# Low-rank attention with layer norm and experts on one core: the query and key weights loaded, turned and absorbed ahead of the first rows

## The reference, cut to what matters

```python
c_q  = h_t @ W_DQ + b_DQ            # 2048 x 32
c_kv = h_t @ W_DKV + b_DKV          # 2048 x 32
q = concat(c_q @ W_UQ + b_UQ, c_q @ W_QR + b_QR)     # per head 128 + 32
k = concat(c_kv @ W_UK + b_UK, h_t @ W_KR + b_KR)    # per head 128 + 32
attn = softmax(q k^T / sqrt(160));  o = attn (c_kv @ W_UV + b_UV);  o @ W_O + b_O
```

## Time and profile before

| what | us |
|---|---|
| median of 3 runs (741.02 to 744.94) | 742.61 |
| the profiled execution, its own time | 741.52 |
| its span, first to last instruction | 739.8 |
| TensorE busy | 718.5 (97%) |
| VectorE busy | 626.1 (85%) |
| GpSimd busy | 581.8 (79%) |
| ScalarE busy | 464.1 (63%) |

### The profile page before, as it was taken

How to read it: one execution, slowest core, us unless ns; L and a number is a source line. 1 busy time by engine, 2 the same in 40 slices (tenths; PEclk the granted TensorE clock), 3 DMA queues, 4 the chain that set the end, 5 groups by cost and what they waited for, 6 DMA issues and landing times.

```text
span 739.8 us, 12509 instructions
## 1 busy us (share of the span) xinstructions
PE 718.5 (97%) x4183; PEld 470.0 (64%) x4183; DVE 626.1 (85%) x1304; ACT 464.1 (63%) x1068; POOL 581.8 (79%) x484
## 2 busy tenths in 40 slices
PE   8999999999999999999999999999799999999997
PEld 7665655655655655655656555466466699778885
DVE  7889999999999999999999999766878636876785
ACT  4367766766766766766767766745677832454553
POOL 6489989999999999999989989954589851445664
PEclk9999999999999999999999999999999999999999
DMA  6300000000000000000000000021000000010330
GB/s 147 90 1 2 1 2 2 2 3 2 1 2 2 1 2 3 1 1 2 2 2 3 1 2 2 1 83 37 1 1 1 1 1 2 0 68 21 114 101 28
DMA packets 39575, 13.72 MB, mean 19 GB/s; under 512 B 27092, under 2 KB 36325, under 8 KB 39512
## 3 DMA queue, kind: packets, MB, share of 16 engines
q1 hardware_dynamic: 38232, 12.81, 7.2%
q10 hardware_dynamic: 1280, 0.12, 0.1%
HBM read 11.52 MB, written 1.08 MB: 17 GB/s over the span
## 4 chain that ended last, share of the span: by engine, by line
PE 69%; POOL 14%; issue 9%; DVE 6%; ACT 1%; DMA 0%; POOLq 0%; DVEq 0%
PE ps L1474 17%; PE ps L1460 15%; PE ps L1518 15%; POOL hid_lo L1000 7%; PE ps L1502 4%; PE ps L1869 4%; PE ps L1529 3%; POOL nrm L982 2%; DVE mx L1054 2%; POOL hid L982 1%; PE ps L1447 1%; PE ps L1448 1%; POOL part L899 1%; POOL sel L976 1%; PE ps L342 1%
## 5 line engine op out<-in xcount | busy, mean ns | idle before, releaser
L1054 DVE TENSOR_REDUCE mx<-ps 128x1 f32<-128x512 f32 x492 | 302.9, 683 | 15.2 <-PE ps L1460 13.7
L621 ACT ACTIVATE prob<-ps 128x512 f32<-128x512 f32 x512 | 262.2, 633 | 9.2 <-PE ps L1474 9.1
L1474 PE MATMUL ps<-q_cols,key 128*128 128x512 f32 x512 | 209.6, 413 | 0.7 <-ACT prob L621 0.7
L1460 PE MATMUL ps<-key,q_rows 128*128 128x512 f32 x512 | 204.2, 403 | 0.8 <-DVE key L1040 0.4
L899 POOL TENSOR_TENSOR part<-part,prob 128x512 f32<-128x512 f32 x124 | 158.4, 1287 | 29.8 <-DVE part L1069 25.3
L1474 PEld LDWEIGHTS ps<-q_cols,key 128*128 128x128 f32 x512 | 95.6, 188 | 90.4 <-issue 50.7
L1518 PE MATMUL ps<-prob,val 128*32 128x512 f32 x1024 | 124.1, 599 | 0.0
L1460 PEld LDWEIGHTS ps<-key,q_rows 128*128 128x128 f32 x512 | 95.7, 188 | 21.2 <-DVE mx L1054 4.1
L899 POOL TENSOR_TENSOR part<-part,pair 128x512 f32<-128x512 f32 x64 | 95.9, 1498 | 0.1
L1000 POOL TENSOR_TENSOR hid_lo<-hid,hid_hi 128x512 fp32r<-128x512 f32 x44 | 60.2, 1377 | 41.6 <-ACT hid_hi L783 41.6
L899 POOL TENSOR_TENSOR pair<-prob 128x512 f32<-128x512 f32 x64 | 82.6, 1291 | 1.9 <-ACT prob L621 1.8
(11 more groups left out here) (285 smaller groups left out, 1171.2 us busy)
## 6 DMA issues: line engine op xcount, KB each, us to landing
den<-den_sb SPq DMA_DIRECT2D x124, 2.0 KB, 2.1
g_all<-g_rows SPq DMA_DIRECT2D x7, 256.0 KB, 3.2
X<-in_L_attn_h_t_dram SPq DMA_DIRECT2D x4, 256.0 KB, 4.4
out_dram<-X SPq DMA_DIRECT2D x4, 256.0 KB, 2.7
g_all<-g_rows SPq DMA_DIRECT2D x4, 224.0 KB, 3.1
w_raw<-in_L_ffn_w_g_dram SPq DMA_DIRECT2D x1, 704.0 KB, 4.4
w_raw<-in_L_ffn_w_u_dram SPq DMA_DIRECT2D x1, 704.0 KB, 6.1
w_raw<-in_L_ffn_w_d_dram SPq DMA_DIRECT2D x1, 704.0 KB, 8.0
```

Of the source, the lines that this page charges most:

```text
L621: act.activation(prob[:, g % RING, :], ps[:, g % 3, :], ACT.Exp, scale=SCALE).then_inc(s_exp, 1)
L1054: dve.tensor_reduce(mx[:, n % 2, c % TPB, at:at + 1], ps[:, BANK["rows", 2 * lin + j], :], AX.X, ALU.max).then_inc(s_mrd, 1)
L1460: pe.matmul(ps[:, BANK["rows", 2 * lin + j], :], q_rows[:, k, i * P:(i + 1) * P], key[:, h % KBUF, c0:c0 + BLK], start=True, stop=True).th ...
L1474: pe.matmul(ps[:, g % 3, :], key[:, n // NB % KBUF, t * P:(t + 1) * P], q_cols[:, n % NB, :], start=True, stop=True).then_inc(s_sc, 1)
```

## The change

The loads of the query and key weights and their biases (4 DMAs) go from SP's queue to the head of ScalarE's; the seven small loads of b_kk and unit go from ScalarE's queue to SP's. On SP's queue the four loads of qr_at now stand behind the second block of X, ahead of the third and fourth. TensorE spins 10 times instead of 14, then turns and absorbs the weights, and only then turns the first rows; rows_T(3) stands between keys(0) and keys(1). ScalarE and VectorE follow that order. On VectorE, absorbed_lo(0), queries_lo(0) and key_biases(0) now come ahead of norm(3) and latents_lo(1). GpSimd's program is the same. Line numbers from L529 to L548 move by up to 6, and all behind them by one.

```diff
@@ -437,16 +437,22 @@
                     sp.dma_start(t[0:C, :], d[f"L0_attn_W_{name}"]).then_inc(signal, 16)
                     sp.dma_start(t[C:C1, :], row(f"L0_attn_b_{name}")).then_inc(signal, 16)
 
+                def load_cols(dst, name):
+                    sp.dma_start(dst, d[name].rearrange("(n a) -> n a", a=1)).then_inc(ld_p, 16)
+
                 load_x(0)
                 load_x(1)
-                load_x(2)
-                load_heads(uq, "UQ", ld_u)
-                load_x(3)
-                load_heads(uk, "UK", ld_u)
                 sp.wait_ge(s_zero, 1)
                 for r in (C, 3 * C):
                     sp.dma_start(qr_at[0:C, :, r:r + C], d["L0_attn_W_QR"].rearrange("c (h r) -> c h r", h=H)).then_inc(ld_q, 16)
                     sp.dma_start(qr_at[C:C1, :, r:r + C], d["L0_attn_b_QR"].rearrange("(a h r) -> a h r", a=1, h=H)).then_inc(ld_q, 16)
+                load_x(2)
+                load_x(3)
+                for r in (0, 2 * C):
+                    load_cols(b_kk[r:r + C, 0:1], "L0_attn_b_DKV")
+                    load_cols(b_kk[r + C:r + 2 * C, 0:1], "L0_attn_b_KR")
+                for r in range(0, SH, C):
+                    load_cols(unit[r:r + C, B_CQ:B_CQ + 1], "L0_attn_b_DQ")
                 load_heads(uv, "UV", ld_w)
                 sp.dma_start(b_v[:, :], row("L0_attn_b_DKV").to_broadcast([P, C])).then_inc(ld_w, 16)
                 sp.dma_start(w_o[:, :, :], d["L0_attn_W_O"].rearrange("(h k) n -> k h n", h=H)).then_inc(ld_w, 16)
@@ -528,21 +534,16 @@
                 def load(dst, src, signal):
                     act.dma_start(dst, src).then_inc(signal, 16)
 
-                def col(name):
-                    return d[name].rearrange("(n a) -> n a", a=1)
-
                 def twice(name):
                     return d[name].unsqueeze(1).to_broadcast([P, 2, C])
 
+                for t, name in ((uq, "UQ"), (uk, "UK")):
+                    load(t[0:C, :], d[f"L0_attn_W_{name}"], ld_u)
+                    load(t[C:C1, :], d[f"L0_attn_b_{name}"].rearrange("(a n) -> a n", a=1), ld_u)
                 halves = w_kk[:, :].rearrange("p (a c) -> p a c", a=2)
                 load(halves[:, :, 0:C], twice("L0_attn_W_DKV"), ld_k)
                 load(halves[:, :, C:2 * C], twice("L0_attn_W_KR"), ld_k)
                 load(w_cq[:, 0:SH].rearrange("p (a c) -> p a c", a=3), d["L0_attn_W_DQ"].unsqueeze(1).to_broadcast([P, 3, C]), ld_k)
-                for r in (0, 2 * C):
-                    load(b_kk[r:r + C, 0:1], col("L0_attn_b_DKV"), ld_p)
-                    load(b_kk[r + C:r + 2 * C, 0:1], col("L0_attn_b_KR"), ld_p)
-                for r in range(0, SH, C):
-                    load(unit[r:r + C, B_CQ:B_CQ + 1], col("L0_attn_b_DQ"), ld_p)
 
                 act.wait_ge(s_const, 2)
                 act.activation(warm[:, :], ident[0:1, 0:1], ACT.Exp)
@@ -620,18 +621,18 @@
                         act.wait_ge(s_sum, ADDS * n)
                     act.activation(prob[:, g % RING, :], ps[:, g % 3, :], ACT.Exp, scale=SCALE).then_inc(s_exp, 1)
 
+                act.wait_ge(s_zero, 3)
+                weights_T(0)
+                weights_T(1)
                 rows_T(0)
+                absorbed_hi(0)
                 rows_T(1)
                 act.wait_ge(s_bkm, 1)
                 act.wait_ge(s_bias, 1)
                 latents_hi(0, 0)
-                act.wait_ge(s_zero, 3)
-                weights_T(0)
-                weights_T(1)
+                queries_hi(0, 3)
                 latents_hi(1, U)
-                queries_hi(0, 3)
                 rows_T(2)
-                absorbed_hi(0)
                 rows_T(3)
                 act.wait_ge(s_kb, 2)
                 keys_hi(0, 3)
@@ -1115,14 +1116,14 @@
                 norm(1)
                 norm_stats(3)
                 norm(2)
+                absorbed_lo(0)
                 dve.wait_ge(s_bkm, 1)
                 dve.wait_ge(s_bias, 1)
                 latents_lo(0, 0)
+                queries_lo(0, 3)
+                key_biases(0, 6)
                 norm(3)
                 latents_lo(1, U)
-                queries_lo(0, 3)
-                absorbed_lo(0)
-                key_biases(0, 6)
                 keys_lo(0, 3)
                 keys_lo(1, 5)
                 latents_lo(2, 0)
@@ -1556,30 +1557,30 @@
                     last.then_inc(s_den_ps, 1)
 
                 pe.wait_ge(s_const, 2)
-                spin(14, U)
-                rows_T(0)
-                pe.wait_ge(ld_k, 16 * N_LD_K)
-                pe.wait_ge(s_zero, 2)
-                pe.wait_ge(s_hT, 1)
-                latents(0, 0)
-                rows_T(1)
+                spin(10, U)
                 pe.wait_ge(ld_u, 16 * N_LD_U)
                 weights_T(0, uq)
                 weights_T(1, uk)
-                pe.wait_ge(s_hT, 2)
-                latents(1, U)
-                queries(0, 3)
-                rows_T(2)
+                pe.wait_ge(s_zero, 2)
                 pe.wait_ge(s_wT, 2)
                 pe.wait_ge(s_place, 1)
                 pe.wait_ge(ld_q, 16 * N_LD_Q)
                 absorbed(0)
+                rows_T(0)
                 key_biases(0, 6)
-                rows_T(3)
+                pe.wait_ge(ld_k, 16 * N_LD_K)
+                pe.wait_ge(s_hT, 1)
+                latents(0, 0)
+                rows_T(1)
+                queries(0, 3)
+                pe.wait_ge(s_hT, 2)
+                latents(1, U)
+                rows_T(2)
                 pe.wait_ge(s_wal, 1)
                 pe.wait_ge(s_kk, 1)
                 pe.wait_ge(s_cq, 1)
                 keys(0, 3)
+                rows_T(3)
                 pe.wait_ge(s_kk, 2)
                 keys(1, 5)
                 pe.wait_ge(ld_w, 16 * N_LD_W)
```

## The result

The changed kernel takes 750.0 us in the median of 4 executions (749.58 to 752.65), the kernel before 741.82 in the median of its 4: the ratio is 1.0112, with a 95% interval from 1.0084 to 1.0139. The profiled execution took 749.58 us; its span is 747.9 us, 8.1 more than before. It is slower, as forecast (749.0, range 745.0 to 752.0).

The account below looks back on a forecast made before the run. TensorE, busy 378.63 of 380 us, bounds the main loop, so only its start moves. rows(0) comes at 27.6 instead of 21.21: 742.6 + 6.4 = 749.0 us, range 745.0 to 752.0.

Parts of the forecast that it names:

- signs that the prediction named: Timeline marks: norm(3)'s four last some 6 us, keys_hi(0) near 25, rows(0) between 27 and 28; queries_lo(0) near 16.7.
- The moment T: End of queries_lo(0) on VectorE, after which GpSimd's series starts; predicted at 16.7 us through weights, row blocks and biases.
- the step that counted four spins at nothing: TensorE's start: 10 spins instead of 14 cost nothing, because they ran while TensorE waited.
- the rival in which T slips as well: Preparation: late biases or TensorE at the spin's slow pace add some 2 us, giving 751.0; chance 15%.
- the main case: Five GpSimd instructions come ahead of norm(3)'s end; 749.0 us, give or take 1.3; chance 56%.
- The other form of that rival, late biases: SP's queue: the seven biases land late, by slower issue or longest landing; some 2 us, within the shared 15%.
- T + 7.3: Predicted end of norm(3) on VectorE: 0.13 + 6.83 + 0.3 us behind queries_lo(0)'s end, at 24.0.
- One such VectorE instruction passes for each GpSimd instruction: Preparation: norm(3)'s four wait in turn for GpSimd's fill, two maskings and cast, lasting some 6 us.
- The bound question: Whether GpSimd's masking holds back a VectorE tensor_scalar: taken as yes; if not, 3.5 us less, 745.5, chance 14%.
- From norm(3) to rows(0): Stretch through rows_T(3), ScalarE's copy and keys_hi(0): from 24.0 to 27.6 us, making rows(0) 6.4 later.
- the three terms: End of queries_lo(0) at 16.7, norm(3)'s end 7.3 us later, then the stretch to rows(0) at 27.6.
- The rival in which norm(3) gets through: VectorE: norm(3) runs in 1.1 us directly behind kcol_m, rows(0) at 21.8, time 743.2; chance 13%.

Follow-up runs that it names:

- the filling: Changed kernel plus 3 spins behind the turned weights and 15 spins between keys(0) and rows_T(3): 747.12 us, ratio 1.0070 to the kernel before.
- two more moves: Changed kernel with norm(3) behind norm(2), 14 spins, key_biases(0) ahead of latents_lo(0), rows_T(3) ahead of keys(0): 741.56 us, ratio 0.9990.
- the pause filled: The version with two more moves, plus 5 spins between the turned weights and absorbed(0): 739.81 us, ratio 0.9960 to the kernel before.

## Why the prediction was right, point by point

**The mechanism holds.** norm(3), moved behind queries_lo(0), meets GpSimd's series; TensorE and ScalarE wait for it. The move alone reproduces most of the loss (ratio 1.0093), and taking GpSimd's series away from beside it restores 1.10 us with VectorE's order unchanged. The shares do not simply add up: put into the kernel before, the move costs 6.9 us; taken out of the changed kernel, it gives back 4.7. Two of the signs that the prediction named did not come. The four were to last some 6 us and lasted 3.12; queries_lo(0) was not to end far from 16.7 and ended at 19.09.

**The moment T, predicted at 16.7, was 19.1.** The missing 2.4 us is the step that counted four spins at nothing: in the profiled execution the changed kernel turned and absorbed the weights at half pace, 3.55 us instead of 1.78. With 14 spins T was 16.5. In the kernel before, the same four spins fewer cost 3.9 us of the median, though not in each execution. But the spins are not the whole of it: with 14 of them, two later profiles show absorbed(0) slow as well. I had this as the rival in which T slips as well, at 15% and 2 us. It belonged in the main case. The other form of that rival, late biases, did not occur: they landed 1.6 to 2.9 us after issue, not 4.8, and were masked by 11.7.

**norm(3) ended at T + 4.1, not T + 7.3.** "One such VectorE instruction passes for each GpSimd instruction" was the step that failed. It holds near 480 us, where GpSimd's additions follow each other without a pause. In this series each GpSimd instruction waits on a semaphore for the one ahead, and 0.06 to 0.08 us pass. At the end of the copy kcol_m and one of the four ended, at the end of the fill two, at the end of the first masking the last. That more get through because of these pauses is my reading; no run was made for it. The length of a pause does not set their number either: with norm(3) late in the kernel before, three ended with the fill and only one with the first masking, though another stood right behind it. The bound question, whether a masking holds VectorE back, was answered as I took it: the last of the four ended with the first masking.

**From norm(3) to rows(0): 5.7 us, not 3.6.** I had priced this stretch at the clock of before. The 2.1 us more are the clock after the wait, shown by the filling, which makes the stretch 3.5. A wait on TensorE costs more than its length, and I left that out.

**The sum.** Measured less predicted, the three terms are +2.4, -3.2 and +2.1 us, together +1.4 before rounding: rows(0) at 28.96 instead of 27.6. The total was near by luck, because the error in one term stood against those in the two others. Two small errors beside the sum also met. I let both kernels run alike behind rows(0), but the clock stayed at 0.50 until 31 us, so the offset grew from 7.75 at rows(0) to 8.55 at the loop's start. And I started from 742.6, where the median of four executions of before is 741.82.

**The rest.** The queues cost nothing, as costed (ratio 1.000). X's late blocks were not late. The offset at the loop's start, 8.55 us, arrived at the end as 8.1, so the loop passed it on. The rival in which norm(3) gets through is out. The early weights show no gain even with the wait removed (1.0008). Where the pace held and two more moves were made, rows(0) came 1.23 us ahead of before; which part of that the early weights have was not separated.

The Trainium skill, "SBUF — State Buffer", section "Who interferes with whom", names the exclusion of the two engines and that the order of issue decides who waits. By that rule the trace agrees for fill, copy and masking alike. It does not show it for every GpSimd instruction: beside the power of rstd_of (L822, 7.54 to 8.68 us in the changed kernel) the four of norm(0) last 343 to 358 ns each, as if undisturbed.

## What to carry to other kernels

Where VectorE works on SBUF data in short tensor_scalar instructions, look at what GpSimd does in the same microseconds: an instruction of 0.3 us can last 1.5. Put it ahead of the signal that sets GpSimd off, or GpSimd's work elsewhere. When TensorE's order gains a pause, price the products behind it at either clock, and do not count spins as free because nothing reads them.

## What the runs showed of the hardware that was not expected

- In the changed kernel TensorE stood idle from 19.9 to 23.3 us, and the granted clock reads 0.50 from 21 to 31 us. Behind the shorter idle time of the version with GpSimd's series later (1.3 us) it reads 0.50 from 22 to 27 us; behind those of 0.8 us with norm(3) early it stayed at 1.00. The length of the pause alone does not decide: with the new queues alone TensorE was idle for 1.94 us ahead of its first transposes at 8.34, and the clock reads 1.00 from 9 to 20 us.
- The same instructions at the same place ran fast in one profile and at half pace in another. absorbed(0) behind 14 spins took 1.86 us where the spin had ended at 6.36 us, and 3.49 where it had ended at 7.18; in the version with two more moves it took 3.48 behind a spin that ended at 7.18, and with the pause filled 1.86 behind one that ended at 6.43. The spin started at 1.58 in all of them. The times of norm(3) early with 14 spins fall into two groups of five, 2.5 us apart. With five spins in a pause of 1.3 us only 1 of 13 lay over 740.4, and that one lost its time elsewhere.
- Where TensorE had once run fast, the clock column followed its pace: 0.51 beside the slow absorbed(0) with norm(3) early, 0.50 in the kernel before with 10 spins. Beside slow products ahead of the first fast ones it reads 1.00, in the spin as in absorbed(0) of the changed kernel.
- Small DMAs on SP's queue, behind X, landed in 1.6 to 2.9 us; on ScalarE's queue, issued beside the loads of X, the same seven had taken 4.6 to 5.1.

Left open: why the granted clock reads 1.00 beside the slow products at the start, what sets the moment at which the spin reaches full pace, and how many VectorE instructions get through at the end of a GpSimd instruction. No run was made for any of them.
